# Spectral filter of a two-block network: real and imaginary parts on the rows of one operand, row transform and second layer on pairs of 64-column tiles

## The chip, the cores and the metric

One Trainium2 chip, of which the kernel uses one core: TensorE (PE; its weight loads are listed apart as PEld), VectorE (DVE), ScalarE (ACT), GpSimd (POOL), and SyncE (SP), whose queue issues the DMAs. The metric is the time of one launch on the device in microseconds (us), the median over runs.

## The reference

Input is one map of 48 x 48 positions with 192 channels. A first block does attention over all 2304 positions (12 heads, with relative positions in rows and columns) and an MLP. A second block normalises, filters in the frequency domain, normalises again and does an MLP. What matters here is the filter:

```python
xf = jnp.fft.rfft2(x.astype(jnp.float32), axes=(1, 2), norm='ortho')
xf = xf.reshape(B, H, Wf, NB, BS)            # H = 48 rows, Wf = 25 columns, 8 blocks of 24 channels
xs = xf[:, total_modes - kept:total_modes + kept, :kept]      # all of them here
xr, xi = (jnp.real(xs), jnp.imag(xs))
o1r, o1i = cmul_add(xr, xi, w1, b1)          # complex product with a 24 x 24 matrix per block, plus bias
o1r, o1i = (jax.nn.relu(o1r), jax.nn.relu(o1i))
o2r, o2i = cmul_add(o1r, o1i, w2, b2)
o2r, o2i = (softshrink(o2r, LAM), softshrink(o2i, LAM))
...
out = jnp.fft.irfft2(full.reshape(B, H, Wf, C), s=(H, W), axes=(1, 2), norm='ortho')
return out.astype(x.dtype) + bias
```

`cmul_add` is `outr = ar*wr - ai*wi + br`, `outi = ai*wr + ar*wi + bi`. All of the filter is computed in float32.

## The kernel before

Every engine has its own instruction stream, written out in order; semaphores are the only link between them. There is no planner: the order in the code is the order in each queue.

**Stages.** Normalisation and projections; products of the queries with the position tables, stored to DRAM; 12 attention heads; the first MLP in 6 chunks of 384 positions (`block0`) with the transform along the map's width in between (`dft`); the filter; the second MLP (`block1`).

**The attention heads.** A head (`period`) goes over three thirds of the queries (`NQ = 3`). For each third SyncE issues nine loads that fill one of two buffers `qv` (`load_qv`, L548 to 567, 1.5 MB together). The last row of `qv` is minus the maximum of each query's scores: DVE makes it (`mneg`), SyncE writes it to DRAM and reads it back (`m_through_dram`, L573 and L575). TensorE starts the scores of the next third (L1065, operands `qv` and `ka`) when the nine loads and this row have landed. After the row's read SyncE issues loads for the next heads (`load_k`, `load_c`), and in the heads 1 and 2 also the constants of later stages: `load_weights` and `load_transforms` in head 1, `load_filters` twice in head 2. All of these stand in one queue, ahead of the next `load_qv`. Every constant load runs through the helper `load` (L334).

**The filter.** The 25 columns of the spectrum are done in `G = 5` groups of `KG = 5`. For a group:

- SyncE loads `f_in` (L691), two DMAs: 96 partitions (48 rows x real, imaginary), five columns x 192 channels. Two groups are loaded ahead; the load for group g + 2 is issued when `transform(g)` is done, and in SyncE's order it stands behind the store of group g - 1 (`f_store`) and ahead of that of group g.
- TensorE, `transform` (L1379): transform along the map's rows. The data is the stationary operand (96 channels), the 96 x 96 matrix `dft_h` the moving one: 10 matmuls of 96 columns. ACT copies the result to `f_x` (L1020), channels on partitions, real and imaginary parts in columns.
- TensorE, `layer1` (L1389): for two halves of the channels and both parts, two matmuls of 240 columns that are added up in PSUM, one with the real and one with the imaginary weights; `f_wn` holds minus the imaginary weights, made by ACT at L974. ACT adds the bias and takes relu into `f_a` (L1037, four instructions).
- DVE makes `f_r` from `f_a` with parts exchanged and one negated (L1611, L1612).
- TensorE, `layer2` (L1400): `f_a` and `f_r` are stationary, the weights moving: 20 matmuls of 96 columns. They write banks 4 to 6 of PSUM.
- DVE adds the bias (L1614, L1617) and does the soft shrinkage (L1619, L1622) into `f_o`.
- TensorE, `inverse` (L1411): three matmuls of 384, 384 and 192 columns, to the same banks 4 to 6. ACT copies to `f_u` (L1027, L1029), SyncE stores it (L697).

TensorE's order in the loop of L1423 is: layer 1 of g, inverse of g - 1, transform of g + 1, layer 2 of g. Before and behind the stage `stay_awake` runs matmuls on unused data.

On the page of this kernel a float32 matmul has two records, each with its own weight load. "96*96 96x240" is a stationary operand of 96 partitions x 96 columns and a moving one of 96 partitions x 240 columns.

Of the kernel before, what the change touches and what calls it, by code (L numbers as in the profile page):

```python
# [29 lines left out]
ds = bass.ds  # L30
# [36 lines left out]
G = KF // KG  # L67
EPS = 1e-5
# [43 lines left out]
def build(nc, d, out):  # L112
    ctx = ExitStack()
    with ctx:
# [40 lines left out]
        f_w = sb("f_w", [C2, 2, 2, 2, C2])  # L155
        f_wn = sb("f_wn", [C2, 2, C2])
        f_b1 = sb("f_b1", [C2, 2, 2])
        f_b2 = sb("f_b2", [2 * S, C])
# [48 lines left out]
        f_x = sb("f_x", [C2, 2, KG, 2, S])  # L207
        f_a = sb("f_a", [C2, 2, KG, 2, S])
        f_r = sb("f_r", [C2, 2, KG, 2, S])
        f_y = sb("f_y", [2 * S, KG, C])  # L210
        f_c = sb("f_c", [2 * S, KG, C])
        f_o = sb("f_o", [2 * S, KG, C])
# [3 lines left out]
        u_sb = sb("u_sb", [4 * KF, CT, C])  # L216
        w_up.append(sb("w_up1", [C2, 2, 2, HID], F16))
        w_dn.append(sb("w_dn1", [128, 2, HM, C], F16))
        xnt_f = sb("xnt_f", [C2, 2, CW])
        y_sb = sb("y_sb", [T, CT, C])  # L220
        f_in = sb("f_in", [2 * S, 2, KG, C])
# [87 lines left out]
        fr_ok = sem("fr_ok")  # L309
# [60 lines left out]
        ALL_CONSTS = 16 * (2 + 4 + 2 + 4 + 3 + 1 + 2 + 2 * NB)  # L370
# [92 lines left out]
        def _(sp):  # L463
# [225 lines left out]
            def f_load(g):  # L689
                for r in range(2):  # L690
                    sp.dma_start(f_in[r * S:(r + 1) * S, g % 2, :, :],  # L691
                                 u1_d[:, r, ds(g * KG, KG), :]).then_inc(f_in_ok[g % 2], 16)
# [49 lines left out]
        def _(pool):  # L742
# [20 lines left out]
            norm_root(pool, nc, rstd, ln1, 1)  # L763
            pool.wait_ge(mask_in, 16)
# [74 lines left out]
            chunks(block0)  # L839
            skip(NC - 1)  # L840

# [16 lines left out]
        def _(act):  # L858
            act.wait_ge(exponent, 1)
            nc.scalar.activation(f_wn[:, 0, 0:CT], rstd[:, 2, :], ACT.Copy)  # L860
# [113 lines left out]
            nc.scalar.activation(f_wn[:, :, :], f_w[:, 0, :, 1, :], ACT.Copy, scale=-1.0).then_inc(fw_neg, 1)  # L974
# [42 lines left out]
            def f_transformed(g):  # L1017
                act.wait_ge(fh_ps, g + 1)
                wait_used(act, f1_ps, g)
                nc.scalar.activation(f_x[:, :, :, :, :].rearrange("p a k r h -> p a (k r h)"),  # L1020
                                     ps[0:C2, 0:2, 0:KG * 2 * S], ACT.Copy).then_inc(fx_ok, 1)

            def f_inverse(g):
                act.wait_ge(fi_ps, g + 1)
                wait_used(act, fu_out, 32 * g)

                nc.scalar.activation(f_u[:, 0:4, :].rearrange("p (a b) c -> p a (b c)", a=2),  # L1027
                                     ps[0:2 * S, 4:6, 0:2 * C], ACT.Copy)
                nc.scalar.activation(f_u[:, 4, :], ps[0:2 * S, 6, 0:C], ACT.Copy).then_inc(fu_ok, 1)  # L1029

            f_transformed(0)
            for g in range(G):
                act.wait_ge(f1_ps, g + 1)
                wait_used(act, f2_ps, g)
                for k in range(2):
                    for r in range(2):
                        ins = nc.scalar.activation(  # L1037
                            f_a[:, k, :, r, :],
                            ps[0:C2, 2 + k, r * KG * S:(r + 1) * KG * S].rearrange("p (k h) -> p k h", h=S),
                            ACT.Relu, bias=f_b1[:, r, k:k + 1])  # L1040
                ins.then_inc(fa_ok, 1)
                if g > 0:
# [701 lines left out]
```

## Time and profile before

| | |
|---|---|
| median of 3 runs | 1104.05 us (1102.33 to 1107.9) |
| span of the profiled execution, first to last instruction | 1100.7 us (its own device time is not listed beside it) |
| TensorE busy | 1025.5 us, 93% |
| weight loads | 722.5 us, 66% |
| VectorE busy | 858.4 us, 78% |
| ScalarE busy | 700.7 us, 64% |
| GpSimd busy | 146.3 us, 13% |
| mean granted clock of TensorE | 0.958 of full speed |
| DMA | 112.80 MB, one queue with 50.5% of 16 engines' span |

Busy shares are means over stages with different bounds. The attention heads fill the stretch from about 110 to 811 us, the first MLP that up to 936, the filter that from 944 to 1003. A profile's "idle before ... <- X" names what ended an engine's wait.

### The profile page before, as it was taken

The page shows a single profiled execution, that of the slowest core. Times are in us where ns is not written, and L with a number is a line of the kernel's source. Part 1 is how long each engine was busy: PE and PEld are TensorE (multiplying, and loading weights), DVE is VectorE, ACT ScalarE, POOL GpSimd, SP SyncE. Part 2 cuts the span into 40 slices and gives each one's busy share as a digit, 9 for nine tenths or more (in the row PEclk, how much of TensorE's full clock was granted, in tenths as well). Part 3 has the DMA queues.
Part 4 walks back from the last instruction along what each step waited for, and adds up shares of the span by engine and source line. Part 5 has one row for each costly group of instructions (what it writes and reads, how often), then busy time and mean ns, then how long its engine had stood idle before and what let it go on. Part 6 is the DMA issues. An engine that isn't in the chain of part 4 may idle for free.

```text
span 1100.7 us, 35778 instructions
## 1 busy us (share of the span) xinstructions
PE 1025.5 (93%) x15498; PEld 722.5 (66%) x15498; DVE 858.4 (78%) x1744; ACT 700.7 (64%) x1003; POOL 146.3 (13%) x118
## 2 busy tenths in 40 slices
PE   5876889999999999999999999999998988998998
PEld 3555155666767676777676768677657775685665
DVE  5757978899999999999999999999626766132564
ACT  4666066677878777777787777777773542231654
POOL 4430000910000000000000000000024553000111
PEclk9975589999999999999999999999999999999999
DMA  5698977666576665666556656655400100222231
GB/s 129 169 233 283 250 135 136 101 118 116 94 115 106 101 109 96 107 99 108 97 106 101 106 99 106 100 91 93 78 16 1 45 22 24 52 68 66 83 87 55
DMA packets 87970, 112.80 MB, mean 102 GB/s; under 512 B 14333, under 2 KB 80194, under 8 KB 87621
## 3 DMA queue, kind: packets, MB, share of 16 engines
q1 hardware_dynamic: 87813, 110.51, 50.5%
q8 instruction: 122, 2.00, 0.9%
q14 instruction: 35, 0.29, 0.1%
HBM read 87.26 MB, written 23.21 MB: 100 GB/s over the span
## 4 chain that ended last, share of the span: by engine, by line
PE 73%; DVE 10%; DMA 7%; ACT 4%; issue 3%; POOL 2%; SPq 0%; DVEq 0%; ACTq 0%
PE ps L1065 37%; PE ps L1225 18%; PE ps L1060 15%; DVE mx_p L1527 3%; DVE xh L101 2%; POOL rstd L109 1%; ACT hid_f L992 1%; PE ps L1078 1%; DVE stage_lo L1496 1%; DMA rel_d<-stage_lo 1%; DVE stats L88 1%; DMA rel<-in_c_rel_w 1%; PE ps L1171 1%; DMA m_d<-mneg 1%; DMA u_sb<-u_d 1%
## 5 line engine op out<-in xcount | busy, mean ns | idle before, releaser
L1527 DVE TENSOR_REDUCE mx_p<-ps 128x1 f32<-128x464 f32 (+1 forms) x1080 | 608.2, 627 | 34.4 <-PE ps L1065 24.8
L942 ACT ACTIVATE prob<-ps 128x768 f32<-128x768 f32 x648 | 495.9, 810 | 186.7 <-PE ps L1065 186.0
L1065 PE MATMUL ps<-kc,qc 112*32 112x464 f16 (+1 forms) x4320 | 460.8, 370 | 8.7 <-issue 5.3
L1065 PE MATMUL ps<-qv,ka 113*32 113x384 f16 x5184 | 404.3, 329 | 9.1 <-DMA qv<-m_d 6.7
L1225 PE MATMUL ps<-prob,v_ext 128*32 128x384 f32 x2592 | 294.5, 488 | 3.4 <-issue 2.7
L1065 PEld LDWEIGHTS ps<-qv,ka 113*32 113x32 f16 x5184 | 213.7, 97 | 85.4 <-issue 27.3
L1065 PEld LDWEIGHTS ps<-kc,qc 112*32 112x32 f16 x4320 | 173.1, 96 | 108.3 <-DVE mx_p L1527 28.2
L1225 PEld LDWEIGHTS ps<-prob,v_ext 128*32 128x32 f32 x2592 | 116.7, 111 | 20.4 <-issue 5.1
L1060 PE MATMUL ps<-xnt_all,w_up 96*128 96x384 f16 x432 | 75.0, 326 | 2.8 <-ACT hid_f L992 2.8
L1060 PE MATMUL ps<-w_dn,hid 128*96 128x192 f16 (+1 forms) x756 | 69.5, 252 | 7.9 <-DVE hid L1582 5.6
L1060 PEld LDWEIGHTS ps<-w_dn,hid 128*96 128x96 f16 (+1 forms) x756 | 65.2, 116 | 13.0 <-DVE hid L1582 6.4
L785 POOL COPY v_ext<-v_all 128x288 f32<-128x288 f32 x12 | 5.0, 425 | 477.9 <-PE ps L1225 477.8
L992 ACT ACTIVATE hid_f<-ps,b_up 128x384 f32<-128x384 f32 x72 | 40.4, 578 | 40.5 <-PE ps L1060 40.5
L1060 PEld LDWEIGHTS ps<-xnt_all,w_up 96*128 96x128 f16 x432 | 41.4, 98 | 34.2 <-ACT hid_f L992 5.5
L109 POOL TENSOR_TENSOR rstd<-rstd 96x4 f32<-96x4 f32 x24 | 27.1, 1128 | 247.1 <-DVE rstd L96 246.7
L1505 DVE TENSOR_TENSOR xnt_all<-xnt_f,xnt_all 96x768 f16<-96x768 f32 x12 | 12.7, 1060 | 40.8 <-ACT xnt_all L934 40.8
L930 ACT ACTIVATE xnt_f<-ps,shift,gain 96x384 f32<-96x384 f32 x24 | 14.7, 661 | 44.4 <-PE ps L1078 44.4
L1496 DVE TENSOR_TENSOR stage_lo<-ps,stage_hi 96x864 f16<-96x864 f32 x32 | 31.1, 1045 | 11.0 <-ACT stage_hi L916 11.0
L916 ACT ACTIVATE stage_hi<-ps 96x864 f16<-96x864 f32 x32 | 27.3, 896 | 15.3 <-PE ps L1060 7.2
L986 ACT ACTIVATE hid<-hid_f 128x384 f16<-128x384 f32 x72 | 35.9, 516 | 0.0
L1582 DVE TENSOR_TENSOR hid<-hid_f,hid 128x384 f16<-128x384 f32 x48 | 26.8, 586 | 10.7 <-ACT hid L986 10.7
L1078 PE MATMUL ps<-ident,xh 96*96 96x96 f32 x144 | 17.1, 268 | 15.7 <-DVE xh L101 15.7
(109 smaller groups left out, 841.7 us busy)
## 6 DMA issues: line engine op xcount, KB each, us to landing
qv<-rel_d SPq DMA_DIRECT2D x216, 144.0 KB
qv<-kq_d SPq DMA_DIRECT2D x108, 216.0 KB
qc<-rel_d SPq DMA_DIRECT2D x24, 216.0 KB, 4.1
xin<-in_x SPq DMA_DIRECT2D x12, 288.0 KB, 3.4
kq_d<-khl SPq DMA_DIRECT2D x24, 144.0 KB, 3.1
q_h<-kq_d SPq DMA_DIRECT2D x9, 288.0 KB, 5.2
q_w<-qw_d SPq DMA_DIRECT2D x9, 288.0 KB, 6.9
rel_d<-stage_hi SPq DMA_DIRECT2D x4, 648.0 KB, 9.6
```

What stands on the lines that cost most here:

```text
L109: nc.gpsimd.tensor_tensor(rstd[:, 1, :], rstd[:, 0, :], rstd[:, 2, :], ALU.pow).then_inc(sem["rstd"], 1)
L916: nc.scalar.activation(out_hi[0], x, ACT.Copy).then_inc(op_hi, 1)
L942: nc.scalar.activation(prob[:, s4(p, s), :].rearrange("p (a b) -> p a b", a=2), ps[:, 3 + 2 * (s % 2):5 + 2 * (s % 2), 0:CW], ACT.Exp).the ...
L986: nc.scalar.activation(hid[:, m, 0, :], hid_f[:, m, :], ACT.Copy).then_inc(sems["hi"], 1)
L992: nc.scalar.activation(hid_f[:, m, :], ps[:, m % 2, 0:CW], ACT.Gelu, bias=b_up[i][:, m:m + 1], scale=1 / WS).then_inc(sems["act"], 1)
L1060: return nc.tensor.matmul(o, l, r, start=start, stop=stop)
L1065: ins = nc.tensor.matmul(ps[c:c + 32, bank, 0:w], l[:, c:c + 32], r, start=True, stop=True, tile_position=(0, c))
L1078: ins = nc.tensor.transpose(ps[0:C2, bank + k, t * T:(t + 1) * T], src[:, t, k * C2:(k + 1) * C2], ident[0:T, 0:T])
L1225: ins = nc.tensor.matmul(ps[r:r + 32, 7, 0:CW], v_ext[:, p, (s + e) % GS, :], prob[:, s4(p, s + e), j * CW:(j + 1) * CW], start=(s % GS == ...
L1496: nc.vector.tensor_tensor(out_lo, x, out_hi, ALU.subtract).then_inc(op_lo, 1)
L1527: nc.vector.tensor_reduce(mx_p[:, q * GT + k // MP, k % MP:k % MP + 1], ps[:, slot, 0:min(MW, N - k % MP * MW)], AX, ALU.max).then_inc(uni ...
L1582: nc.vector.tensor_tensor(hid[:, m, 1, :], hid_f[:, m, :], hid[:, m, 0, :], ALU.subtract).then_inc(sems["lo"], 1)
```

## The change

Real and imaginary parts are put on partitions 0 to 47 and 64 to 111 of one operand (`FR = 64` is the start of the second part, `FP = 112` the height), and the channels are handled in four groups of `FC = 48`. Layer 1 then needs no sum over parts: one matmul of 240 columns per channel group, four in all. Transform and second layer make both halves of the rows with a pair of matmuls on two tiles of TensorE, 64 columns wide (`tile_position=(0, r * 64)`), 40 matmuls of 48 columns each; the stationary slice has 64 columns, of which the last 16 reach into the next data or a pad. `f_r` and DVE's two copies are gone. The inverse is two matmuls of 480 columns and writes banks 6 and 7. In TensorE's and ACT's loops the transform of g + 1 now stands ahead of the inverse of g - 1. The tables and weights get more and smaller loads: in `load_transforms` 12 bias and table loads stand behind the first three in place of 3, and each call of `load_filters` has 24 in place of 8. GpSimd has memsets for the pads.

```diff
@@ load_transforms, load_filters
             load(eng, dft_h[:, :, :], d["c_dft_h"])
-            load(eng, f_b1[:, :, :].rearrange("p r k -> p (r k)"), d["f_b1"].rearrange("r (k p) -> p (r k)", p=C2))
+            eng.wait_ge(fw_zero, 4)
             for r in range(2):
-                load(eng, f_b2[r * S:(r + 1) * S, :], d["f_b2"][r:r + 1, :].to_broadcast([S, C]))
+                load(eng, dft_hi[r * FR:r * FR + S, :], d["c_dft_h"][r * S:(r + 1) * S, 1, :])
+                load(eng, f_b1[r * FR:r * FR + FC, :], d["f_b1"][r:r + 1, :].rearrange("o (g p) -> p (o g)", p=FC))
+                for g in range(FG):
+                    load(eng, f_b2[r * FR:r * FR + S, g, :, :],
+                         d["f_b2"][r:r + 1, g * FC:(g + 1) * FC].unsqueeze(1).to_broadcast([S, KG, FC]))
...
-            eng.wait_ge(fw_zero, 1)
+            eng.wait_ge(fw_zero, 4)
             for b in range(NB):
-                p0 = (b % 4) * BS
-                load(eng, f_w[p0:p0 + BS, layer, b // 4, :, p0:p0 + BS],
+                p0 = (b % 2) * BS
+                load(eng, f_w[p0:p0 + BS, layer, b // 2, :, p0:p0 + BS],
                      d["f_w"][layer, :, b].rearrange("r k o -> k r o"))
+                for r in range(2):
+                    load(eng, f_w[FR + p0:FR + p0 + BS, layer, b // 2, r, p0:p0 + BS], d["f_w"][layer, 1 - r, b])
@@ gpsimd
+            nc.gpsimd.memset(dft_hi[:, :], 0.0).then_inc(fw_zero, 1)
+            nc.gpsimd.memset(f_b1[:, :], 0.0).then_inc(fw_zero, 1)
+            nc.gpsimd.memset(f_b2[:, :, :, :], 0.0).then_inc(fw_zero, 1)
+            pool.wait_ge(fw_zero, 4)
...
+            for b in range(2):
+                nc.gpsimd.memset(f_in[:, b, KG * C:KG * C + FPAD], 0.0)
             skip(NC - 1)
+            nc.gpsimd.memset(f_a[:, 2 * FN:2 * FN + FPAD], 0.0).then_inc(f_pads, 1)
@@ scalar
-            nc.scalar.activation(f_wn[:, :, :], f_w[:, 0, :, 1, :], ACT.Copy, scale=-1.0).then_inc(fw_neg, 1)
+            for layer in range(2):
+                ins = nc.scalar.activation(f_w[FR:FP, layer, :, 0, 0:FC], f_w[FR:FP, layer, :, 0, 0:FC], ACT.Copy,
+                                           scale=-1.0)
+            ins.then_inc(fw_neg, 1)
...
             def f_inverse(g):
...
+                for a in range(2):
+                    ins = nc.scalar.activation(
+                        f_u[:, :, a * 2 * FC:(a + 1) * 2 * FC].rearrange("p f (g c) -> p g f c", g=2),
+                        ps[0:2 * S, 6 + a, 0:FN].rearrange("p (g f c) -> p g f c", g=2, f=KG), ACT.Copy)
+                ins.then_inc(fu_ok, 1)
...
+                if g + 1 < G:
+                    f_transformed(g + 1)
                 if g > 0:
                     f_inverse(g - 1)
-                if g + 1 < G:
-                    f_transformed(g + 1)
@@ tensor
-                for k in range(2):
+                for j in range(FG):
                     for f in range(KG):
-                        ins = mm(ps[0:C2, k, f * 2 * S:(f + 1) * 2 * S], f_in[:, g % 2, f, k * C2:(k + 1) * C2],
-                                 dft_h[:, 0, :])
+                        x = f_in[:, g % 2, f * C + j * FC:f * C + j * FC + FR]
+                        col = j % 2 * KG * S + f * S
+                        for r in range(2):
+                            ins = nc.tensor.matmul(ps[r * FR:(r + 1) * FR, j // 2, col:col + S], x,
+                                                   dft_h[:, 0, r * S:(r + 1) * S], start=True, stop=True,
+                                                   tile_position=(0, r * FR))
...
             def layer1(g):
...
+                for j in range(FG):
+                    cols = slice(j % 2 * KG * S, (j % 2 + 1) * KG * S)
+                    ins = mm(ps[0:FP, 2 + j // 2, cols],
+                             f_w[:, 0, j, :, :].rearrange("p r c -> p (r c)")[:, 0:FP], f_x[:, j // 2, cols])
...
             def layer2(g):
-                pe.wait_ge(fr_ok, g + 1)
-                wait_used(pe, fu_ok, g)
...
+                pe.wait_ge(fa_ok, g + 1)
+                wait_used(pe, fy_ok, g)
+                for j in range(FG):
+                    for f in range(KG):
+                        col = j % 2 * KG * FC + f * FC
+                        x = f_a[:, j * KG * S + f * S:j * KG * S + f * S + FR]
+                        for r in range(2):
+                            ins = nc.tensor.matmul(ps[r * FR:(r + 1) * FR, 4 + j // 2, col:col + FC], x,
+                                                   f_w[:, 1, j, r, 0:FC], start=True, stop=True,
+                                                   tile_position=(0, r * FR))
...
             def inverse(g):
                 pe.wait_ge(fo_ok, g + 1)
...
+                wait_used(pe, fu_ok, g)
+                for a in range(2):
+                    ins = mm(ps[0:2 * S, 6 + a, 0:FN], dft_hi[:, :], f_o[:, a, :])
...
+            pe.wait_ge(f_pads, 1)
             transform(0)
             for g in range(G):
                 layer1(g)
+                if g + 1 < G:
+                    transform(g + 1)
                 if g > 0:
                     inverse(g - 1)
-                if g + 1 < G:
-                    transform(g + 1)
                 layer2(g)
@@ vector
-                nc.vector.tensor_scalar(f_r[:, :, :, 0, :], f_a[:, :, :, 1, :], -1.0, None, ALU.mult)
-                nc.vector.tensor_copy(f_r[:, :, :, 1, :], f_a[:, :, :, 0, :]).then_inc(fr_ok, 1)
                 dve.wait_ge(f2_ps, g + 1)
-                nc.vector.tensor_tensor(f_y[:, 0:4, :].rearrange("p (a b) c -> p a b c", a=2),
...
+                nc.vector.tensor_tensor(f_y[:, :, :], ps[0:FP, 4:6, 0:FN],
+                                        f_b2[:, :, :, :].rearrange("p (a g) f c -> p a (g f c)", a=2),
+                                        ALU.add).then_inc(fy_ok, 1)
```

## Rows read from the trace of the kernel before

**Rows 1.** Chain that ended last, 940 to 1010 us: start us, us, what.
```profile
944.16 1.92 PE ps L1060 x20
...
952.96 39.13 PE ps L1060 x308
...
1003.03 0.30 SPq L697
```
**Rows 2.** Timeline, filter stage, TensorE: start us, us, engine line op out<-in xcount.
```profile
950.45 1.86 PE L1060 MATMUL ps<-dft_h,f_in 96*96 96x96 f32 x20
...
952.96 0.41 PE L1060 MATMUL ps<-f_w,f_a 96*96 96x96 f32 x2 [0.65 <-DVE f_r L1612]
...
956.43 0.57 PE L1060 MATMUL ps<-f_x,f_w 96*96 96x240 f32 x2
...
959.79 1.86 PE L1060 MATMUL ps<-f_o,dft_h 96*96 96x384 f32 x6
```
**Rows 3.** Groups of weight loads by shape, whole span: busy us, mean ns of one.
```profile
L1171 PEld LDWEIGHTS ps<-sel,o_sb 128*32 128x32 f32 x864 | 21.1, 109 | 8.7 <-issue 1.5 <-DVE mx_p L1527 0.6
...
L1060 PEld LDWEIGHTS ps<-f_w,f_a 96*96 96x96 f32 x100 | 12.5, 165 | 2.3 <-DVE f_r L1612 2.3
```
**Rows 4.** Timeline and (last row) group by shape: from whole array to column groups.
```profile
818.10 0.33 PE L1060 MATMUL ps<-xnt_all,w_up 96*128 96x384 f16 x1
...
818.35 0.46 PE L1171 MATMUL ps<-sel,o_sb 128*32 128x34 f32 x24
...
855.45 2.11 PE L1060 MATMUL ps<-xnt_all,w_up 96*128 96x384 f16 x12
...
L1171 PE MATMUL ps<-sel,o_sb 128*32 128x34 f32 x864 | 18.5, 197 | 0.0
```
**Rows 5.** Groups of DVE and ACT, filter stage.
```profile
L1622 DVE TENSOR_TENSOR f_o<-f_y,f_c 96x960 f32<-96x960 f32 x5 | 5.8, 1155 | 0.2
...
L1619 DVE TENSOR_SCALAR f_c<-f_y 96x960 f32<-96x960 f32 x5 | 3.3, 656 | 0.2
...
L1020 ACT ACTIVATE f_x<-ps 96x960 f32<-96x960 f32 x5 | 4.8, 966 | 11.0 <-PE ps L1060 11.0
```
**Rows 6.** Timeline of SyncE, filter stage, and landing times of the `f_in` loads.
```profile
962.73 0.77 SPq L697 DMA_DIRECT2D u_d<-f_u  x2
963.54 1.02 SPq L691 DMA_DIRECT2D f_in<-u_d  x2
...
DMA to landing us min/median/max: 2.9/3.2/3.6
```
**Rows 7.** Timeline of SyncE, head 1, around `load_transforms`.
```profile
244.04 2.52 SPq L334 DMA_DIRECT2D f_b<-in_f_b  x3
246.60 1.37 SPq L567 DMA_DIRECT2D qv<-kq_d  x3
```
**Rows 8.** Timeline of SyncE, head 2, around `load_filters`.
```profile
282.03 1.30 SPq L567 DMA_DIRECT2D qv<-kq_d  x3
...
294.68 0.70 SPq L575 DMA_DIRECT2D qv<-m_d  x1
...
298.15 3.29 SPq L334 DMA_DIRECT2D f_w<-in_f_w  x8
301.49 1.30 SPq L567 DMA_DIRECT2D qv<-kq_d  x3
```
**Rows 9.** Stretch: us, busy (x) of PE, PEld, DVE, ACT, POOL, PEclk, DMA share, GB/s.
```profile
303.00:312.00 9.00, 9.00 (x198) 5.53 (x191) 8.77 (x19) 6.64 (x9) 0.00 (x0) 1.00 1.07 160
```
**Rows 10.** Chain that ended last, 240 to 264 us.
```profile
255.61 3.53 DMA m_d<-mneg
...
259.15 2.37 DMA qv<-m_d
```
**Rows 11.** Timeline of TensorE: first scores of two thirds of head 2.
```profile
298.55 0.61 PE L1065 MATMUL ps<-qv,ka 113*32 113x384 f16 x8
...
317.08 0.49 PE L1065 MATMUL ps<-qv,ka 113*32 113x384 f16 x7
```

More of the change, by code:

```diff
@@ L67 @@
 G = KF // KG
+FC = 2 * BS
+FG = C // FC
+FR = 64
+FP = FR + FC
+FN = FG // 2 * KG * S
+FPAD = FR - FC
 EPS = 1e-5
@@ L154, in build @@
         dft_h = sb("dft_h", [2 * S, 2, 2 * S])
[L155 to L158, printed above, removed]
+        dft_hi = sb("dft_hi", [FP, 2 * S])
+        f_w = sb("f_w", [FP, 2, FG, 2, FR])
+        f_b1 = sb("f_b1", [FP, FG])
+        f_b2 = sb("f_b2", [FP, FG, KG, FC])
+        table_in = sb("table_in", [T, CT])
         with ExitStack() as r:
@@ L206, in build @@
             hid_f = sb("hid_f", [128, HM, CW], F32, r)
[L207 to L212, printed above, removed]
+        f_x = sb("f_x", [FP, 2, FN])
+        f_a = sb("f_a", [FP, 2 * FN + FPAD])
+        f_y = sb("f_y", [FP, 2, FN])
+        f_c = sb("f_c", [FP, 2, FN])
+        f_o = sb("f_o", [FP, 2, FN])
         f_u = sb("f_u", [2 * S, KG, C])
@@ L308, in build @@
         fa_ok = sem("fa_ok")
-        fr_ok = sem("fr_ok")
+        f_pads = sem("f_pads")
         f2_ps = sem("f2_ps")
@@ L690, in f_load @@
                 for r in range(2):
[L691 to L692 removed]
+                    sp.dma_start(f_in[r * S:(r + 1) * S, g % 2, 0:KG * C],
+                                 u1_d[:, r, ds(g * KG, KG), :].rearrange("h f c -> h (f c)"))\
+                      .then_inc(f_in_ok[g % 2], 16)
             def f_store(g):
@@ L859, in _ @@
             act.wait_ge(exponent, 1)
-            nc.scalar.activation(f_wn[:, 0, 0:CT], rstd[:, 2, :], ACT.Copy)
+            nc.scalar.activation(table_in[:, :], rstd[:, 2, :], ACT.Copy)
             act.wait_ge(first_in, FIRST)
@@ L1019, in f_transformed @@
                 wait_used(act, f1_ps, g)
-                nc.scalar.activation(f_x[:, :, :, :, :].rearrange("p a k r h -> p a (k r h)"),
-                                     ps[0:C2, 0:2, 0:KG * 2 * S], ACT.Copy).then_inc(fx_ok, 1)
+                nc.scalar.activation(f_x[:, :, :], ps[0:FP, 0:2, 0:FN], ACT.Copy).then_inc(fx_ok, 1)
             def f_inverse(g):
@@ L1034, in _ @@
                 wait_used(act, f2_ps, g)
-                for k in range(2):
[L1036 to L1040, printed above, removed]
+                for j in range(FG):
+                    w = KG * S
+                    ins = nc.scalar.activation(f_a[:, j * w:(j + 1) * w],
+                                               ps[0:FP, 2 + j // 2, j % 2 * w:(j % 2 + 1) * w],
+                                               ACT.Relu, bias=f_b1[:, j:j + 1])
                 ins.then_inc(fa_ok, 1)
+                if g + 1 < G:
+                    f_transformed(g + 1)
                 if g > 0:
                     f_inverse(g - 1)
-                if g + 1 < G:
-                    f_transformed(g + 1)
             f_inverse(G - 1)
@@ L1412, in inverse @@
                 pe.wait_ge(fo_ok, g + 1)
-                for j in range(-(-KG // 2)):
-                    w = min(2, KG - 2 * j)
-                    ins = mm(ps[0:2 * S, 4 + j, 0:w * C], dft_h[:, 1, :],
-                             f_o[:, 2 * j:2 * j + w, :].rearrange("p f c -> p (f c)"))
+                wait_used(pe, fu_ok, g)
+                for a in range(2):
+                    ins = mm(ps[0:2 * S, 6 + a, 0:FN], dft_hi[:, :], f_o[:, a, :])
                 ins.then_inc(fi_ps, 1)
```

28 lines of the change are left out of this document (4 added, 24 removed).

## The prediction

> **What bounds the kernel now.** The groups of instructions put most of the time in the attention heads, where TensorE has no idle time: in a stretch of 9 us it is busy 9.00 us, at granted clock 1.00 [rows 9]. What delays TensorE there delays the end by as much. The filter stage was read next, in the chain that ended last. It runs from the first row transform at 944.16 to the store of the last group at 1003.03, 58.9 us; one piece of it is 39.13 us of TensorE alone, 308 records [rows 1]. So there TensorE's own instructions are the bound, and DVE and ACT count only at the ends. Per group (one group is five columns of the spectrum) the timeline of TensorE gives 40 records of the second layer from 952.96 to 956.43 (0.087 us each), 16 of the first from there to 959.79 (0.21 each; a moving operand of 240 columns takes 0.20 for its two passes, I use 0.205), 6 of the inverse in 1.86 us and 20 of the transform in 1.86 us, of which 0.25 is the end of the last one: 0.085 each [rows 2]. A float32 matmul is two records. The sum is 1.7 + 3.3 + 1.6 + 3.4 = 10.0 us.
> Last I read SyncE's queue where the edited load functions issue: at 244.04 (three loads of biases) and at 298.15 (eight loads of filter blocks, and the same eight at 278.7) [rows 7, 8], and the chain near them: the last row of the scores' operand goes through DRAM, its write took 3.53 us at 255.61 and its read 2.37 us, and TensorE waited for it [rows 10].
>
> **The filter stage, part by part.** The first layer goes from 8 matmuls to 4 of the same 240 columns: 8 records x 0.205 = 1.64 us for 3.3. The inverse goes from three matmuls (384, 384, 192 columns) to two of 480, 960 columns in both: still 1.6 us. The transform goes from 10 matmuls of 96 columns to 40 of 48, the second layer from 20 of 96 to 40 of 48; both as 20 pairs, the two of a pair on different column groups of the array, so 40 rounds of two records each.
> What is a round? From below, the matmul alone: 48 columns, two passes, half of the 0.085 of 96 columns, 0.0425 us. From above, the pair costs what a 96-column record costs, 0.085, if neither narrower operand helps; and two such one after the other if the column groups don't overlap. For overlap speaks the one row with float32 on column groups: 24 records of 34 columns with 32-column weights on three groups take 0.46 us, of which 0.20 is the last one's own length [rows 4]: 0.26 us for 8 rounds, 0.033 each. Between them stands the weight load. A load of 96 columns is recorded as 165 ns, one of 32 as 109 [rows 3]: 0.875 ns a column, so 56 ns for 64 columns, longer than the 42.5 ns of the matmul under which it has to hide; padding 48 columns to 64 costs that. I take 0.057 us a round: transform 2.3 us (0.6 more than now), second layer 2.3 us (1.1 less).
> The trace shows that a load runs under the matmul before it on the same rows of the array: with 0.084 us for a 96-column load and 0.08 for the matmul, records still start 0.087 apart [rows 2, 3]. The Trainium skill says the opposite in "TensorE: Matmul & The Clock Gate" (Part 3, what overlaps and what doesn't): a weight load overlaps matmuls in flight only if its row group differs, and all pairs here share all rows. By that rule a round is load plus matmul; it is a rival below.
> Changing between whole array and column groups is new, four times a group. At 818 the first narrow record starts at 818.35, 0.25 us after a record of 384 columns whose like follow each other at (2.11 - 0.33) / 11 = 0.16: 0.09 us a change [rows 4], 0.4 us a group.
> New group: 1.64 + 2.3 + 1.6 + 2.3 + 0.4 = 8.2 us for 10.0.
> Dependencies: the transform now stands ahead of the inverse. The load for group g+2 is issued behind the store of group g, so it leaves after the inverse and ACT's copy: store 0.77 us, loads 1.02 us, and the second of these lands 3.2 us after its issue [rows 6]; from the end of ACT's copy that is some 4.6 us. Now the transform waits for it: copy of group 0 ends at 16.7 us of the stage, its data lands at 21.3, TensorE is there at 19.5. Twice such a wait of 1.8 us (groups 3 and 4; group 2 is loaded early). DVE's three steps take 1.16 + 0.66 + 1.16 + small gaps = 3.05 us after the second layer [rows 5], the subtraction of the bias being one piece of 960 now; under first layer and transform they hide in 4 us, in the last group, without a transform, only under 1.64: 1.4 us of waiting. Gone are two DVE copies (off the path, the transform hid them) and the wait of the last second layer for ACT (1.2 us), since the inverse has banks of its own.
> Laid out in order (first transform 2.3, copy 1.0, five first layers, four more transforms, five second layers, five inverses, 18 changes, waits 3.6 + 1.4, the tail of DVE 3.05, inverse 1.8 and ACT's copy 1.0, [rows 5]): 50.8 us for 58.9, **-8.0 us**. With 0.0425 a round it is 46.2 us (-12.6; longer waits for the load eat part), with 0.085 59.8 (+1).
> The relus, four a group, stay as they are. At nothing I cost ACT's two small negations in the attention stage for one (ACT waits for TensorE in every step there) and GpSimd's new memsets (some at its start, some after its last addition before the stage, while TensorE waits for the loads): a few tenths of a us if that cover is gone.
>
> **The queue in the attention stage.** The edit turns 3 bias loads into 12, and twice 8 filter loads into 24. Each costs SyncE an issue: 0.41 us in the row of eight (3.29 us and the gap to the next, 3.34 / 8) [rows 8]; for the bias loads I take 0.45 to 0.48. Behind them in the same queue stand the nine loads of the next third of a head, 1.5 MB, and behind those the write and read of the maxima row. With the transfers full (DMA share 1.07 over 303 to 312 [rows 9]) that last write is not through until they are: at 246.60 the nine begin, at 259.15 the read is issued, 12.55 us later, and 2.37 us on TensorE can go [rows 7, 10].
> A: bias loads, 9 x 0.45 = 4.0 less part of a stall that is already in the 2.52 us of three: 3.5 us. TensorE waited there already [rows 10]: all of it passes, +3.5.
> B: 16 x 0.41 = 6.6 us. The nine begin at 282.03 + 6.6 = 288.6, the read is issued at 301.2 for 294.68, TensorE goes at 303.6 for 298.55 [rows 8, 11]: +5.1.
> C: SyncE comes from B at 301.2, passes the four loads of the next head (3.5 us in [rows 8], 0.9 of them, I estimate, a wait that is then over: 2.6), then 24 x 0.41 = 9.9 to 313.7, + 12.55 = 326.2, + 2.4 = 328.6, for 317.08 [rows 11]: +11.5, of which B had 5.1: +6.4.
> Sum **+15.0 us**. TensorE is full, so nothing is caught up. Lower end: issue 0.32 for a small load, 2 + 3.6 + 4.9 = 10.5; lowest, 0, if the transfers could be squeezed. Upper: 19.
>
> **Sum.** +15.0 - 8.0 = +7 on the profiled span of 1100.7 us, 1107.7; the runs' median of 1104.05 lies 3.35 above the span, so **1111 us**.
>
> **Rivals.**
> 1. The queue costs nothing. Other thirds of a head have 1 to 2 us between the row's arrival and TensorE's need (294.68 + 2.37 = 297.05 for 298.55 [rows 8, 10, 11]); it needs the transfers to be done in the 5 us or so that SyncE idles before the maxima are ready. Against it: the DMA rings are full, and A waits already. Then only -8: 1096, faster.
> 2. The weight load hides and a round is 0.0425: -12.6 + 15 = +2.4, 1106.5, no change.
> 3. Pairs are no faster than 96-column records: 0.085 and +1, with the queue 1120. With load and matmul one after the other (0.056 + 0.042 = 0.098 a round) 64 us, +5: 1124. Against both: rows 2 and 4. What decides is whether the rounds pass 0.082.
> By the rule of the Trainium skill named above the last of these would hold.
>
> **Chances.** Forecast 0.54 (its own range 1105 to 1117: queue 10.5 to 19, round 0.050 to 0.064), rival 1 0.16, rival 2 0.18, rival 3 0.12. The range must take in most of rival 2 and reach the others: 1096 to 1120. Half a per cent, 5.5 us, is about what a measurement can tell here from no change. Faster by more: rival 1, 0.15. Slower by more than that (over 1109.6): most of the forecast and rival 3, 0.55. Within: rival 2 and the low part of the forecast, 0.30.
>
> **What would show it.** Records of the transform and of the second layer 0.057 apart per column group (0.0425: rival 2; 0.085 or more: rival 3). Two waits of TensorE for the group's load near 1.8 us, one of 1.4 for DVE's last step. The nine operand loads starting 3.5, 6.6 and, against TensorE, again 6.6 us later behind the constants; TensorE waiting some 4, 5 and 6 us there for the maxima row. The filter stage 50.8 us, and its start 15 us later than 944. No such waits in the attention stage would make the forecast wrong by its larger term.

## The result, and the profile after

The changed kernel takes 1116.7 us (median of 4 runs, 1110.77 to 1121.9), the kernel before 1103.19 beside it; the difference of the medians is 13.5 us. The ratio is 1.0117 (95% interval 1.009 to 1.0144): slower by 12.9 us, clear of the noise. The profiled execution took 1118.69 us, its span is 1116.9, 16.2 more than before.

The page of the changed kernel, the same parts as in the table of before: busy time, then the granted clock in 40 slices.

```profile
PE 1023.9 (92%) x15948; PEld 714.3 (64%) x15948; DVE 856.0 (77%) x1729; ACT 701.1 (63%) x1004; POOL 147.9 (13%) x124
...
PEclk9885589998989999999999999999999999999999
```

TensorE has less to do than before and the span is longer, so it waits more. The chain that ended last says where, in the heads 1 and 2 (start us, us, what):

```profile
261.53 3.38 DMA m_d<-mneg
...
282.64 3.25 DMA m_d<-mneg
...
304.60 6.94 DMA m_d<-mneg
...
330.90 4.95 DMA m_d<-mneg
```

TensorE at the first scores of these four thirds (in brackets, how long it stood idle before them and what ended that):

```profile
267.40 0.83 PE L1087 MATMUL ps<-qv,ka 113*32 113x384 f16 x8 [5.98 <-DMA qv<-m_d]
...
288.35 0.51 PE L1087 MATMUL ps<-qv,ka 113*32 113x384 f16 x8 [0.37 <-DMA qv<-m_d]
...
314.06 0.83 PE L1087 MATMUL ps<-qv,ka 113*32 113x384 f16 x8 [7.40 <-DMA qv<-m_d]
...
338.31 0.51 PE L1087 MATMUL ps<-qv,ka 113*32 113x384 f16 x8 [3.13 <-DMA qv<-m_d]
```

Four thirds of a head in a row wait for the maxima row. They start 5.7, 7.9, 15.5 and 21.2 us later than in the kernel before (the last two stood at 298.55 and 317.08 [rows 11], the first two at 261.7 and 280.4). The row's read takes 2.3 to 2.4 us each time, its write 3.25 to 6.94 (in the thirds that are on time TensorE waits 0.8 us or less for it). Behind them the distance stays near 20, and the filter begins 19.7 us late. The first eight records after the two longest waits take 0.83 us, where the like take 0.51, and the first eight of the step behind the scores 1.28 for 0.65: they run at the lower of TensorE's two clocks, 1.2 GHz and not 2.4. Granted clock by stretch (us, TensorE busy, then the other engines, then clock, DMA share, GB/s):

```profile
262.00:268.00 6.00, 0.59 (x9) 0.34 (x12) 0.00 (x0) 0.00 (x0) 0.00 (x0) 0.77 0.52 119
268.00:290.00 22.00, 21.63 (x394) 13.19 (x390) 18.84 (x36) 15.44 (x21) 0.43 (x1) 0.91 0.28 74
306.00:316.00 10.00, 2.60 (x33) 1.06 (x28) 1.74 (x4) 1.51 (x2) 0.00 (x0) 0.68 0.70 140
316.00:332.00 16.00, 16.00 (x293) 9.40 (x289) 13.88 (x27) 10.79 (x15) 0.00 (x0) 0.88 0.46 71
```

In the second and fourth stretch TensorE is full and yet short of clock: 0.09 x 22 + 0.12 x 16 = 3.9 us of work lost. Only the first 2.0 of them delay the stage. Behind the second stretch TensorE waits again, 3.13 us, for a row whose write SyncE sends off directly behind its own loads (their issue ends at 330.85, the write goes at 330.90), so this work had time.

The filter stage on TensorE (start us, us, ..., idle before and what ended it):

```profile
969.29 2.54 PE L1410 MATMUL ps<-dft_h,f_in 96*64 96x48 f32 x80
971.65 2.50 PE L1432 MATMUL ps<-f_w,f_a 112*64 112x48 f32 x80
974.09 1.87 PE L1082 MATMUL ps<-f_x,f_w 112*112 112x240 f32 x8
975.89 2.54 PE L1410 MATMUL ps<-dft_h,f_in 96*64 96x48 f32 x80
978.36 1.85 PE L1082 MATMUL ps<-f_o,dft_hi 112*96 112x480 f32 x4
980.14 2.54 PE L1432 MATMUL ps<-f_w,f_a 112*64 112x48 f32 x80
982.61 1.88 PE L1082 MATMUL ps<-f_x,f_w 112*112 112x240 f32 x8
986.17 2.54 PE L1410 MATMUL ps<-dft_h,f_in 96*64 96x48 f32 x80 [1.69 <-DMA f_in<-u_d]
...
997.09 2.89 PE L1410 MATMUL ps<-dft_h,f_in 96*64 96x48 f32 x80 [2.33 <-DMA f_in<-u_d]
999.91 3.12 PE L1082 MATMUL ps<-f_o,dft_hi 112*96 112x480 f32 x4
...
1008.64 1.85 PE L1082 MATMUL ps<-f_o,dft_hi 112*96 112x480 f32 x4 [1.34 <-DVE f_o L1643]
```

From start to start a group costs 1.80 + 2.47 + 1.78 + 2.47 = 8.5 us. Before it cost 10.15, from one first layer at 956.43 [rows 2] to the next at 966.58; the prediction's sum had 10.0. The transform at 969.29 is followed by the second layer without a change to the whole array: 2.36 us for 40 rounds, 0.059 each, and with the change 2.47. Two waits for `f_in`, one for DVE, and behind the second wait a transform and an inverse that take 0.35 and 1.27 us too long. From the first transform (963.88) to the last store (1019.05) the stage takes 55.2 us for 58.9: -3.7. So 16.2 = 19.7 - 3.7 + 0.2.

### The profile page after: what moved, and what is told of

It reads as the page before. It is cut to its first block, busy times and chain, and to the rows that moved or that the text cites. A ratio compares the mean times of both kernels' runs of the same rounds, so it can differ in the third digit from the quotient of the medians.

```text
span 1116.9 us, 36711 instructions
## 1 busy us (share of the span) xinstructions
PE 1023.9 (92%) x15948; PEld 714.3 (64%) x15948; DVE 856.0 (77%) x1729; ACT 701.1 (63%) x1004; POOL 147.9 (13%) x124
## 4 chain that ended last, share of the span: by engine, by line
PE 70%; DVE 11%; DMA 10%; ACT 4%; issue 3%; POOL 2%; SPq 1%; DVEq 0%; ACTq 0%
PE ps L1087 36%; PE ps L1247 17%; PE ps L1082 12%; DVE mx_p L1553 4%; DMA m_d<-mneg 2%; DVE xh L107 1%; DMA qv<-m_d 1%; POOL rstd L115 1%; ACT hid_f L1015 1%; PE ps L1100 1%; DMA rel_d<-stage_lo 1%; DVE stage_lo L1522 1%; PE ps L1410 1%; DMA rel<-in_c_rel_w 1%; DVE stats L94 1%
## 5 line engine op out<-in xcount | busy, mean ns | idle before, releaser
L1087 PE MATMUL ps<-qv,ka 113*32 113x384 f16 x5184 | 404.7, 330 | 25.0 <-DMA qv<-m_d 22.1
L1531 DVE TENSOR_TENSOR xnt_all<-xnt_f,xnt_all 96x768 f16<-96x768 f32 x12 | 12.9, 1072 | 41.0 <-ACT xnt_all L954 41.0
L1636 DVE TENSOR_TENSOR f_y<-ps,f_b 112x960 f32<-112x960 f32 x5 | 5.8, 1158 | 46.6 <-PE ps L1432 46.6
```

The lines of the kernel that those rows point to most:

```text
L1087: ins = nc.tensor.matmul(ps[c:c + 32, bank, 0:w], l[:, c:c + 32], r, start=True, stop=True, tile_position=(0, c))
```

## The experiments

Two columns of the table come from the traces: "heads" is the time from the start of the sixth third of a head to that of the tenth (242.6 to 317.1 before), the four thirds that lie behind the edited loads; "stage" is that from the first transform to the last store. Ratios are to the kernel before. The diffs are shortened: lines with "..." or with words in place of code stand for several. The runs of one kernel lie 7 to 14 us apart and each kernel has one trace, so a difference of a few us between two rows is only as good as the trace that shows where it arises.

| kernel | us, median | ratio (95%) | heads | stage |
|---|---|---|---|---|
| before | 1103 to 1107 | 1 | 74.5 | 58.9 |
| changed | 1116.7 | 1.0117 (1.009 to 1.0144) | 95.7 | 55.2 |
| e1, before + 41 loads | 1133.8 | 1.0256 (1.0227 to 1.0285) | 98.6 | 58.9 |
| e7, changed, bias in 2 loads | 1108.2 | 1.0028 (1.0009 to 1.0047) | 86.5 | 57.3 |
| e9, changed, bias in 8 small loads | 1111.9 | 1.0057 (1.003 to 1.0083) | 90.5 | 52.7 |
| e8, changed, filter blocks spread | 1105.9 | 1.0015 (0.9987 to 1.0042) | 82.7 | 59.1 |
| e11, changed, loads from GpSimd | 1105.5 | 1.0013 (0.9977 to 1.0049) | 75.1 | 57.9 |
| e2, all bundled | 1100.8 | 0.9949 (0.9919 to 0.9979) | 75.2 | 58.0 |
| e5, e2 in the old order | 1097.5 | 0.9917 (0.9884 to 0.9951) | 74.0 | 53.3 |
| e6, e2 + matmuls in the waits | 1095.9 | 0.9896 (0.9834 to 0.9957) | 74.0 | 52.9 |
| e3, e2 + early load | 1091.9 | 0.9863 (0.9802 to 0.9923) | 74.6 | 49.4 |
| e4, e3 + 48-column slices | 1085.8 | 0.9818 (0.9769 to 0.9866) | 73.5 | 45.1 |
| e10, e4, all constants spread | 1090.9 | 0.9853 (0.98 to 0.9906) | 78.2 | 45.1 |

**Is it the queue?** The loads alone, in the kernel before:

```diff
             for r in range(2):
                 load(eng, f_b2[r * S:(r + 1) * S, :], ...)
+            ... 9 loads into extra: 2 tables, 1 of f_b1, 6 of f_b2 times five
@@ load_filters, per block
+                for r in range(2):
+                    load(eng, extra[...], d["f_w"][layer, 1 - r, b])
```

> The kernel before, with nothing of the filter changed, plus 41 small constant loads that nobody reads: 9 behind the bias loads of head 1, 16 behind each of the two sets of filter blocks of head 2. Theory (SyncE's issues delay the next third's nine loads, the maxima row behind them comes late, TensorE waits): the filter stage starts 16 to 21 us later than in the kernel before (which had 944), itself unchanged at 59, the time is 16 to 21 us above the kernel before, with the gaps of TensorE in the thirds that start near 267, 288, 314 and 338 as in the changed kernel. Rival (the later start has to do with something else of the change, GpSimd's memsets or ACT's negations or the layout): below 3 us. Rival (the loads cost SyncE's plain issue time only, 41 x 0.41 less the slack of a third): 10 to 13 us, with no long waits behind the issue.

It is 28 us slower, more than any theory gave; the filter and all behind it are as before. So the queue alone is enough for the loss, and my 16 to 21 was low. Between the traces the four thirds make up 24.0 us; another 5.1 arise ahead of them, where nothing was edited, and their cause is not shown. The trace shows where most of it arises, at the third behind the bias loads: the seven issues took 3.38 us, but then the nine operand loads took 2.68 + 7.54 for their issue (the first three 1.37 before [rows 7], the other six 2.79), and the maxima row's write 9.03 us. SyncE (start us, us, ...) and the chain of waits:

```profile
252.34 3.38 SPq L335 DMA_DIRECT2D extra<-in_f_b  x7
255.77 2.68 SPq L579 DMA_DIRECT2D qv<-kq_d  x3
258.50 7.54 SPq L579 DMA_DIRECT2D qv<-rel_d  x6
```
```profile
266.09 9.03 DMA m_d<-mneg
```

**Issues or bytes, filter blocks and bias together.** e2 brings the same blocks in 8 loads a layer, and the bias once, with copies on chip:

```diff
-            for b in range(NB): ... 3 loads of one block
+            for b in range(2):
+                for r in range(2):
+                    for h in range(2):
+                        load(eng, f_w[h * FR + p0:..., layer, :, r, p0:p0 + BS],
+                             d["f_w"][layer, (r, 1 - r)[h], b::2].rearrange("g k o -> k g o"))
-                for g in range(FG): load(eng, f_b2[..., g, :, :], ... .to_broadcast([S, KG, FC]))
+                load(eng, f_b2[..., :, 0, :], ...)      # GpSimd copies to the other four columns
```

> The changed kernel with fewer loads for the same bytes: the filter blocks in 8 loads a layer, each of four blocks, for 24; the second bias in 2 loads for 8, its five copies made on chip by GpSimd before the filter stage. Theory (the number of issues costs): the attention stage is the kernel before's plus about 1.5 us (three more loads in head 1), the filter stage starts near 946 and takes 55.2 us as in the changed kernel: 1101 to 1104 us, 13 to 17 below the changed kernel, 2 to 3 below the kernel before. Rival (bytes or descriptors of these loads cost, which stay as they are): within 4 us of the changed kernel. In between, 5 to 10 below it, would say that both count.

Heads back at 75.2, start of the filter at 940.5, 1100.8 us: the number of issues is what costs, for the filter blocks. But its stage took 58.0, not 55.2, with more time at a low clock behind a wait for `f_in` (below). Of the 5 us under the kernel before, its trace has 0.9 in the stage and 3.7 ahead of it, most of these in the first MLP, which nothing here touches and which differs by up to 3 us between the traces. So that e2 itself beats the kernel before is measured, but why is not shown.

**The bias alone.** e7 bundles only the bias, e9 keeps its 8 loads but makes each small:

```diff
-                         d["f_b2"][..., g * FC:(g + 1) * FC].unsqueeze(1).to_broadcast([S, KG, FC]))
+                         d["f_b2"][..., g * FC:(g + 1) * FC].to_broadcast([S, FC]))      # e9, into column 0
```

> The changed kernel with only the second bias bundled (2 loads for 8, copies on chip), the filter blocks in 24 loads a layer as there. It leaves 6 loads for 12 in head 1. Theory: the delay of the first two thirds (5.7 and 2.5 us) falls by 3 to 6 us in all, the two sets of filter blocks still cost their 12 to 13: the changed kernel minus 3 to 6. Rival (the loads of head 1 are under cover): no difference. Rival (a late queue in head 1 also starts the delay of head 2): minus more than 8.

> As many loads in head 1 as the changed kernel has (8 for the second bias), but each brings 48 x 48 values once and not five times over (GpSimd makes the copies before the filter stage); filter blocks in 24 loads a layer. With 2 loads in place of 8 the third behind them started 0.6 us later than in the kernel before, in the changed kernel 5.7. Theory (the number of issues): the third behind them starts 4 us or more later than in the kernel before, the time is within 3 us of the changed kernel. Rival (packets: the eight loads of 240 small packets each fill the queue, and later issues stall): below 2.5 us later, and the time is that of the kernel with the bias in 2 loads, 1108, to within 3 us.

SyncE around the bias loads (start us, us, ...), in the changed kernel, in e9, and in e7:

```profile
244.40 3.50 SPq L340 DMA_DIRECT2D f_b<-in_f_b  x5
...
248.44 4.01 SPq L340 DMA_DIRECT2D f_b<-in_f_b  x5
252.49 3.09 SPq L579 DMA_DIRECT2D qv<-kq_d  x3
255.62 5.86 SPq L579 DMA_DIRECT2D qv<-rel_d  x6
261.53 0.33 SPq L585 DMA_DIRECT2D m_d<-mneg  x1
```
```profile
245.35 3.59 SPq L340 DMA_DIRECT2D f_b<-in_f_b  x5
...
249.44 3.25 SPq L340 DMA_DIRECT2D f_b<-in_f_b  x5
252.74 1.37 SPq L579 DMA_DIRECT2D qv<-kq_d  x3
254.15 2.79 SPq L579 DMA_DIRECT2D qv<-rel_d  x6
256.99 0.33 SPq L585 DMA_DIRECT2D m_d<-mneg  x1
```
```profile
245.34 0.91 SPq L340 DMA_DIRECT2D f_b<-in_f_b  x2
246.29 2.49 SPq L578 DMA_DIRECT2D qv<-kq_d  x3
248.83 2.80 SPq L578 DMA_DIRECT2D qv<-rel_d  x6
```

The third behind them starts 5.7, 4.1 and 0.8 us later than in the kernel before, the next one another 2.2, 1.0 and -0.2. So of 7.9 us, 4.5 are six more issues and 2.9 are the five-fold bytes. The ten bias issues take 7.51 us in the changed kernel and 6.84 in e9, the nine operand loads behind them 8.95 and 4.16. Of these 4.8 us little reaches TensorE. DVE has the maxima at 255.59 (256.58 in e9), and in the changed kernel their write stands behind the operand loads until 261.53, but then takes 3.38 us; in e9 it goes at 256.99 and takes 7.1. From the first of the nine to the row's read it is 12.4 us with the five-fold bytes, 11.4 without, 12.55 in the kernel before [rows 7, 10]. The rest of the 2.9 arises in the next third, where TensorE waits 0.37 us in the changed kernel and not in e9, at granted clocks of 0.89 and 0.91.

e9 met neither expectation in time, 4.8 below the changed kernel and 3.7 above e7; both causes count. e7's time is 8.5 below the changed kernel, inside the rival's number (more than 8), and its trace has 7.4 of it in head 1 and 1.8 in head 2: most is the loads' own, and a late queue in head 1 does lengthen head 2.

e7 is also a cleaner measurement of my terms B and C: its thirds behind the filter blocks take 24.3 and 23.8 us for 18.1 and 18.5, +6.2 and +5.3, 11.5 together where I had 11.5.

**Spread.** e8: four of the 48 loads at each of 12 places.

```diff
-            for b in range(NB): ... 24 loads
+            for dst, src in parts[i * 4:i * 4 + 4]:
+                load(eng, dst, src)
@@ period
-                    if is_at(n, 2): load_filters(sp, q - 1)
+                    if 2 <= n <= 7: load_filters(sp, (n - 2) // 3, (n - 2) % 3 * 2 + q - 1)
```

> The changed kernel with the same 48 filter-block loads, not 24 at two places of head 2 but 4 at each of 12 places in heads 2 to 7. The loads of head 1 stay as they are. Theory (a third has 1 to 2 us between the maxima row's arrival and TensorE's need, so 4 issues of 0.41 us fit): of the 21 us by which the filter stage starts late about 8 are left, 13 us below the changed kernel. Rival (each issue costs what it takes, wherever it stands): no gain, within 2 us of the changed kernel. Rival (slack is part of it): every place costs some tenths of a us, 5 to 9 below.

10.8 us below the changed kernel, between the theory's 13 and the second rival's 9. In the trace the heads from there on are as in the kernel before (475.5 us from the tenth third to the attention's last projection, 475.2 before); of the 8.2 that the four thirds keep, 7.5 are head 1's. Four issues a place cost under 1 us in all where 24 at one place cost 5 to 8.

**Another queue.** e11: the 63 loads, one by one, from GpSimd.

```diff
@@ gpsimd
                     copy_v(2 * i + p, p)
+                    if i == 1:
+                        if p == 0: load_transforms(pool)
+                        load_filters(pool, p)
```

> The changed kernel with its 15 loads of transforms and biases and its 48 loads of filter blocks, one by one as there, issued by GpSimd and not by SyncE, between its copies of heads 2 and 3. The bytes and packets stay as they are. Theory (what delays the attention stage is that SyncE's stream is held up by the issues): no third starts late, the filter stage starts some 20 us earlier than in the changed kernel, near 944, and the time is 17 to 21 us below it, 1096 to 1100. Rival (the small packets themselves crowd out the operand loads of the next third): still 8 us or more of the 21. Rival (GpSimd's issues are slow and delay its copies for the heads): waits of TensorE for those copies in heads 2 to 4.

11.2 us below the changed kernel, a little over half of what the theory gave. GpSimd's first 39 loads fell on the operand loads of a third in head 1 that stands close behind SyncE's own twelve weights: those nine took 5.32 and 7.82 us for their issue, the maxima row's write 8.14, and the third started 29.6 us after the one before it, for 20.0 in the kernel before. This third lies ahead of the four that the column "heads" counts. The second 24, at 269.92, delayed nothing. GpSimd, SyncE, and the chain of waits:

```profile
227.27 13.27 POOL L342 DMA_DIRECT2D f_w<-in_f_w  x24
...
269.92 13.24 POOL L342 DMA_DIRECT2D f_w<-in_f_w  x24
```
```profile
223.14 5.32 SPq L582 DMA_DIRECT2D qv<-kq_d  x3
228.51 7.82 SPq L582 DMA_DIRECT2D qv<-rel_d  x6
```
```profile
236.70 8.14 DMA m_d<-mneg
```

So there are two costs: the issuing stream (gone here) and the crowding of the operand loads in flight. Which one a load pays depends on where it stands. What crowds is not separated: the first 39 loads hold the eight bias loads with the five-fold bytes, the 24 that delayed nothing hold none. The filter stage takes 57.9 us here, 2.7 more than in the changed kernel's trace, by the clock (below).

**The filter's order, load and clock.** Three kernels on the base of e2:

```diff
@@ e5, tensor and scalar
-                transform(g + 1); inverse(g - 1)
+                inverse(g - 1); transform(g + 1)
@@ e6, tensor, before transform(3) and transform(4)
+                        pe.wait_ge(fx_ok, g + 1)
+                        stay_awake(8, 0, hid[:, 0, 0, :])
@@ e3, SyncE
-            for g in range(G):
-                if g + 2 < G: wait for transform g; f_load(g + 2)
-                f_store(g)
+            for g in range(-1, G):
+                if g + 3 < G: wait for transform g + 1; f_load(g + 3)
+                if g >= 0: f_store(g)
```

> The kernel with bundled loads, but TensorE and ACT in the order of the kernel before: inverse of g - 1 ahead of the transform of g + 1. Theory: the two waits for the group's load (1.5 and 2.6 us) and the fall of the clock behind the second go, since the transform stands later; in their place the inverse waits 1.34 us for DVE's last step in each of four groups, where it did in one. Stage to the end of the last inverse 49.6 + 3 x 1.34 = 53.6 us; in the bundled kernel it was 58 in its trace, in the others with the new order 53 to 57. So the time is 0 to 4 us below the bundled kernel (1100.8). Rival (the new order hides more than it costs): 3 us or more above it. Rival (the load is late in this order too): no difference, with waits for the load in the trace.

> The kernel with bundled loads, and eight matmuls of 384 columns on unused data ahead of the transforms of groups 3 and 4, where TensorE waits 1.5 and 2.6 us for the group's load. They take 1.3 us of these waits. Theory (the clock falls because TensorE idles there): the load lands as late as before, but the transform, inverse and second layer behind it run at full clock: 2.54, 1.85 and 2.54 us in place of 4.51, 3.52 and 3.33; 3 to 4 us below the bundled kernel. Rival (the fall has another cause, such as the load on the chip at that point): no difference, or slower by the part of the 1.3 us that doesn't fit.

> The kernel with bundled loads, and SyncE issues the load of group g + 3 as soon as transform g + 1 is done, ahead of the wait for the store of group g. Theory (the load is late because it stands behind the store, and the fall of the clock follows from the wait): no wait for the load before the transforms of groups 3 and 4 (1.5 and 2.6 us in the bundled kernel), clock full through the stage, stage 49.5 us to the end of the last inverse in place of 58; the time 6 to 8 us below the bundled kernel, about 1094. Rival (the waits move to ACT or DVE instead): 3 us or less. Rival (the clock falls there anyway): 4 us.

The transform of group 4 and what follows, in e2, e6 and e3, and the windows of 10 us behind the wait in e2 and e6 (us, TensorE busy, granted clock, DMA share, GB/s):

```profile
973.74 4.51 PE L1413 MATMUL ps<-dft_h,f_in 96*64 96x48 f32 x80 [2.55 <-DMA f_in<-u_d]
978.18 3.52 PE L1085 MATMUL ps<-f_o,dft_hi 112*96 112x480 f32 x4
981.63 3.33 PE L1435 MATMUL ps<-f_w,f_a 112*64 112x48 f32 x80
```
```profile
974.66 2.54 PE L1413 MATMUL ps<-dft_h,f_in 96*64 96x48 f32 x80 [0.54 <-DMA f_in<-u_d]
```
```profile
976.97 2.54 PE L1414 MATMUL ps<-dft_h,f_in 96*64 96x48 f32 x80
```
```profile
974.00:984.00 10.00, 10.00 (x138) 0.53 0.06 13
```
```profile
975.00:985.00 10.00, 8.66 (x169) 1.00 0.15 39
```

In e6 the load is nearly as late as in e2 (the transform starts 10.4 us behind the one before, 11.1 in e2), TensorE has something to do meanwhile, and the clock stays at 1.00 where it was 0.53 over the 10 us behind the wait. In e2 the transform, inverse and second layer there take 1.97 + 1.67 + 0.79 = 4.4 us longer than in e6, where they take 2.54, 1.85 and 2.54. The time is 4.9 below e2. One reservation stays: this is one trace, and e9's kept the clock too, without such matmuls, behind waits of 1.55 and 1.56 us.

The fall costs 1.6 us in the changed kernel, 3.2 in e7, 4.4 in e2 and e11, 6.3 in e8 (twice) and nothing in e9. With the length of the wait ahead of it, this is why the stage takes 52.7 to 59.1 us in traces that share its instructions. e3 takes the waits away too: no wait for the load, stage 49.4 (expected 49.5), the time 8.9 below e2 (expected 6 to 8). e5: stage 53.3 (expected 53.6), waits of 1.34 to 1.41 for DVE in each group and none above 0.5 for the load; 3.3 below e2. So the new order gains nothing by itself: it is level with the old one where the clock holds (52.7 for 53.3), loses where it falls (55.2 to 59.1), and gains 4 us once the load is moved (49.4).

**What sets a round.** e4, on e3, from the second group on, in the transform and in the same way in the second layer:

```diff
-                        x = f_in[:, g % 2, f * C + j * FC:f * C + j * FC + FR]
+                        x = f_in[:, g % 2, f * C + j * FC:f * C + j * FC + FC]
```

> The kernel with early loads and, from the second group on, stationary slices of 48 columns where they were 64 (the rows between the two tiles keep what the first group left, and meet rows of zeros in the weights). Theory (the weight load sets the round, 0.9 ns a column): a round falls from 0.0585 to 0.044 us, eight transforms and second layers save 0.58 us each, 4.6 us in all, less what then waits for ACT or DVE (up to 1.5): 3 to 4.6 us below the kernel with early loads, 1090. Rival (the round is set by something that doesn't depend on the columns, two passes in line or the issue of the pair): no difference.

```profile
967.53 2.00 PE L1415 MATMUL ps<-dft_h,f_in 96*48 96x48 f32 x80
969.46 1.85 PE L1086 MATMUL ps<-f_o,dft_hi 112*96 112x480 f32 x4
```
```profile
L1415 PEld LDWEIGHTS ps<-dft_h,f_in 96*48 96x48 f32 x320 | 7.5, 125 | 1.3 <-issue 1.3
...
L1415 PEld LDWEIGHTS ps<-dft_h,f_in 96*64 96x64 f32 x80 | 2.4, 138 | 0.9 <-issue 0.9
```

Forty rounds with their change of mode go from 2.47 to 1.93 us, 13.5 ns a round for 16 columns of the stationary slice, and the loads' records shrink by 13 ns with them; the moving operand is the same. So the weight load sets the round. The stage takes 45.1 us, 4.3 below e3, where 3 to 4.6 were expected of the time. The medians lie 6.1 apart, with overlapping runs. It is 1.8% below the kernel before, the fastest of the versions.

**Spread what is left.** e10, on e4: the 37 constant loads at three per place.

```diff
-                    if is_at(n, 1) and q == 1: load_weights(sp)  ... and the transforms and filter blocks
+                    if n >= 1: load_some(sp, 3)
```

> The kernel with early loads and 48-column slices, and the 37 constant loads of head 1 and 2 (12 weights and biases, 9 transforms and biases, 16 filter blocks) not in four clusters but three at each of 13 places from head 1 on. In the kernel before, the thirds behind the clusters start 20.0, 19.1, 18.7, 18.2 and 18.6 us apart where others are 18.15, some 3.8 us too much. Theory (three issues fit into a third's slack): these go, 3 to 4 us below the kernel with 48-column slices, 1082 to 1083. Rival (the clusters are not what makes these thirds long, the transfers are): within 1.5 us of it. Rival (every place costs some tenths): 1 to 2 us below to 2 above.

No gain: 1090.9, intervals overlap with e4's. Its trace has three thirds 18.1 to 18.2 us apart as the theory wants, then two of 19.7 and 22.1, with a stop of TensorE of 2.31 us inside a third near 305 for which the trace names nothing, and a granted clock of 0.83 in the 10 us from 306 on. One trace can't tell if that belongs to the spreading; left open.

## Why the prediction was right or wrong

The forecast was +7 (1111), measured +12.9 (1116.7), inside the range, by the forecast mechanism: the queue costs more than the stage gives. Both terms were off, in the same direction, and the queue's 21.2 lies above its upper end of 19. That the time still falls within the forecast's own range (1105 to 1117), by 0.3 us, owes something to luck: the profiled run, whose span is 16.2 us longer, is the second slowest of four.

**The queue, +15.0: right in kind, low in size, 21.2.** Term A, +3.5, was mis-sized most: 7.9. I took 3.5 us for nine more issues, and they took 6.0: from the first load of `load_transforms` to the first operand load it is 9.8 us (242.70 to 252.49), 3.8 in the kernel before. That I had [rows 7] with a stall in it already (2.52 for three) should have put A's upper end higher. The time from there to the row's read was as assumed, 12.4 for 12.55, though the issue of the operand loads took 8.95 of it. So 5.7 us reach the first third. The other 2.2 come in the next one, which the forecast left at nothing: its granted clock is 0.89 over 20.95 us, a loss of 2.3.

B and C were 5.1 and 6.4, 11.5 together. They measured 6.2 and 5.3 in e7, where head 1 is nearly clean: the right sum, with luck in it, since two errors cancel. Twenty-four loads took 11.9 and 9.8 us where I had 9.9, and from the operand loads to the row's read it was 11.4 and 10.8 where I had 12.55. In the changed kernel they are 7.6 and 5.7. B is larger there because the third before it starts with its row already late, by 0.37 us of waiting, and the slack of 1.5 us that B may use up in e7 is gone. The clock is not the reason: C's third has 0.88 in the changed kernel and 0.89 in e7. Of the 6.2 us above the forecast, A's issues are 2.2, the clock behind A 2.2, B 2.5 and C -0.7.

**The filter stage, -8.0: -3.7 in this trace.** The round was forecast load-bound at 0.057 us, and it is load-bound (e4), at 0.059. With the change of mode the steady cost is 2.47 for my 2.4, the first layer 1.80 for 1.73, the inverse 1.78 for 1.69: 1.5 us over the stage. The waits for the load were 1.69 and 2.33 for 1.8 twice, 0.4 more, DVE's 1.34 for 1.4. Another 1.6 us is the clock behind the second wait, which I had not in the sum at all, and about 0.8 I can't place. In other traces of the same stage the clock costs 0 to 6.3 us. The list of the layout names the last inverse twice ("five inverses" and "inverse 1.8"); counted once its terms come to 51, so the 50.8 stands.

**Rivals.** That the queue costs nothing (1096): refuted by e1. A round of 0.0425: refuted, 2.36 / 40 = 0.059 with 64 columns; e4 comes to about (1.93 - 0.11) / 40 = 0.046 with 48, close to it. Pairs no faster than 96-column records, or load and matmul in series: refuted, 40 rounds would be 3.4 or 3.9 us. By that the trace disagrees with the rule of the Trainium skill weighed in the prediction ("TensorE: Matmul & The Clock Gate", Part 3, what overlaps and what doesn't), for pairs on column groups in float32: all share their rows, and load and matmul do overlap. The prediction took that rule alone: the same part of the Trainium skill says that a load is also pulled ahead of running matmuls when it goes to the background weight buffer, and with that the 0.059 could agree; no run here shows which of the two loads are.

**At nothing.** ACT's negations and GpSimd's memsets: in the filter stage no engine's wait ends with one of them.

## What to carry over

A constant load of a few KB costs its place in the issuing queue: small loads stand best a few at a time where a stage has slack, or bundled, and a broadcast is made on chip. When a full TensorE is made to wait, add the clock to the wait: a stop of 2.5 us cost up to 4.4 more behind it. In the one trace with eight matmuls on unused data in the stop nothing was lost; moving the load so that there is no stop gave more. When operands get narrower, the load of the stationary slice is the floor; don't pad it.

## What was not expected of the hardware

- Large broadcasts slow the issue of the loads behind them (8.95 us for nine against 4.16) more than their own (7.51 us for ten against 6.84). But the maxima row behind the nine comes only 1.1 us later by it, 12.4 us behind the first of them against 11.4.
- Loads from a second engine are not free for the first: six operand loads beside them took 7.82 us to issue, a small write 8.14 to land.
- Twenty-four loads in a row cost 5 to 8 us, four at each of twelve places under 1 us in all.
- The granted clock fell behind some waits of TensorE in the filter stage and not behind others of the same length: behind 2.33, 2.44, 2.55 and 3.04 us in four traces, behind 1.71 and 1.58 in e8 (transforms of 3.94 and 3.67 us), not behind 1.69 in the changed kernel nor behind 1.55 and 1.56 in e9. Why is open.
